# Two of sixteen dBu products moved from VectorE to GpSimd, and from PSUM to SBUF

## The reference

```python
deltaA = jnp.exp(delta[..., None] * A)                      # 16 units per channel
deltaB_u = delta[..., None] * Bm[:, :, None, :] * xi[..., None]
def step(state, inputs):
    dA_t, dBu_t, C_t = inputs
    state = dA_t * state + dBu_t
    y_t = jnp.einsum('bdn,bn->bd', state, C_t)
    return (state, y_t)
```

## Time and profile before

| | |
|---|---|
| median of 3 runs | 1354.28 us (1354.16 to 1357.81) |
| the profiled execution | 1355.75 us, span 1353.9 us |
| PE busy in the span | 1060.0 us (78%) |
| DVE busy | 932.1 us (69%) |
| POOL busy | 817.2 us (60%) |
| ACT busy | 745.8 us (55%) |
| state space, scans from 535.0 to 1020.9 us | 256 scans, mean 1204 ns |
| dBu products, line 1630 | 256, mean 685 ns |
| products with C on POOL, line 1569 | 256, mean 1273 ns |

### The profile page before, as it was taken

The page is one execution under the profiler, slowest core; times in us unless marked ns, Lnnn a source line. Parts: engine busy times, 40 slices in busy tenths (PEclk is TensorE's granted clock), DMA queues, the critical chain, the costliest instruction groups (busy, mean ns, idle before and its releaser), DMA issues. The chain is left out here.

```text
span 1353.9 us, 20321 instructions
## 1 busy us (share of the span) xinstructions
PE 1060.0 (78%) x4202; PEld 618.8 (46%) x4203; DVE 932.1 (69%) x2276; ACT 745.8 (55%) x1821; POOL 817.2 (60%) x602
## 2 busy tenths in 40 slices
PE   3898874349999955888989888897775319999995
PEld 3666653227777731333333333333223215555563
DVE  4999997503333333799999999989997625555573
ACT  3777754325555547858586776757531115555542
POOL 1443320667317557877886888788781567437276
PEclk9999985569999976989999999899897559999997
DMA  8994000136425425344435443443540026535335
GB/s 243 161 147 139 1 1 1 41 53 88 71 56 89 84 31 110 85 141 133 155 116 168 124 157 124 137 159 114 185 140 1 31 54 94 85 73 96 79 67 103
DMA packets 136875, 133.22 MB, mean 98 GB/s; under 512 B 14578, under 2 KB 117602, under 8 KB 136674
## 3 DMA queue, kind: packets, MB, share of 16 engines
q1 hardware_dynamic: 107106, 115.55, 32.3%
q0 software_dynamic: 29696, 16.86, 9.8%
HBM read 98.66 MB, written 31.60 MB: 96 GB/s over the span
## 5 line engine op out<-in xcount | busy, mean ns | idle before, releaser
L1569 POOL TENSOR_TENSOR ss_HC<-ss_Hs,ss_Cb 128x512 f32<-128x512 f32 x256 | 317.8, 1273 | 92.1 <-PE ss_Y L1343 70.9
L1343 PE MATMUL ss_Y<-ss_HC,g_ident 128*128 128x512 f32 x512 | 268.7, 643 | 45.5 <-POOL ss_HC L1569 38.0
L1638 DVE TENSOR_TENSOR_SCAN ss_Hs<-ss_dA,ss_dBu 128x512 f32<-128x512 f32 x256 | 297.3, 1204 | 7.0 <-ACT ss_dA L1485 7.0
L992 PE MATMUL m_x_UP<-g_m_w,m_x_gT 128*128 (+1 forms) x532 | 203.9, 489 | 5.9 <-issue 2.9
L1485 ACT ACTIVATE ss_dA<-ss_delta,g_A 128x510 f32<-128x510 f32 x256 | 168.0, 714 | 55.3 <-DVE ss_Hs L1638 54.9
L1343 PEld LDWEIGHTS ss_Y<-ss_HC,g_ident 128*128 128x128 f32 x512 | 90.4, 197 | 206.7 <-POOL ss_HC L1569 147.9
L1630 DVE TENSOR_TENSOR ss_dBu<-ss_duP,ss_Bb 128x512 f32<-128x512 f32 x256 | 163.4, 685 | 21.0 <-DMA ss_Bb<-bc_rows 16.8
L1012 PEld LDWEIGHTS m_x_DP<-g_m_w,m_x_hT 128*128 128x128 f32 (+1 forms) x908 | 131.0, 189 | 80.4 <-issue 41.2
L1012 PE MATMUL m_x_DP<-g_m_w,m_x_hT 128*128 (+3 forms) x908 | 161.5, 296 | 5.9 <-ACT m_x_hT L1068 3.4
L1095 DVE SCALAR_TENSOR_TENSOR m_x_hid<-m_x_UP,m_x_G,m_x_sg 128x352 f32<-128x352 f32 x78 | 45.5, 584 | 151.2 <-ACT m_x_sg L1050 147.6
L972 POOL DMA_INDIRECT g_X<-out_rows,g_slot x64 | 99.2, 1550 | 78.4 <-DMA out_rows<-m_x_YO 55.8
(11 more groups left out here) (242 smaller groups left out, 1869.8 us busy)
## 6 DMA issues: line engine op xcount, KB each, us to landing
ss_Bb<-bc_rows SPq DMA_DIRECT2D x64, 512.0 KB, 4.9
ss_Cb<-bc_rows SPq DMA_DIRECT2D x64, 512.0 KB, 4.1
rows<-g_Z SPq DMA_DIRECT2D x2, 5031.0 KB, 54.2
m_x_G<-rows SPq DMA_DIRECT2D x156, 64.5 KB
out_rows<-m_x_YO SPq DMA_DIRECT2D x156, 64.0 KB
g_m_w<-in_w_up SPq DMA_DIRECT2D x1, 2816.0 KB, 10.7
g_m_b<-in_b SPq DMA_DIRECT2D x1, 2160.0 KB, 11.2
g_X<-in_x SPq DMA_DIRECT2D x4, 512.0 KB, 5.8
```

The source lines that it names most:

```text
L992: ins = nc.tensor.matmul(UP[v % 2][:, at:at + n], gT[v % 2][:], w.w[:, ds(e + c, n)], start=True, stop=True)
L1343: ins = nc.tensor.matmul(Yp[:, h, :], ident[:], HC[n % 2][:, h, :], start=False, stop=n == N - 1)
L1569: nc.gpsimd.tensor_tensor(HC[n % 2][:, h, :], Hs[n % 4][:, h, :], Cb[g % 2][:, n % 2, :], ALU.mult).then_inc(hc_ready.sem, 1)
L1638: v_.tensor_tensor_scan(Hs[n % 4][:, h, :], dA[n % NA][:, h, :, :].rearrange("p s t -> p (s t)"), dBu[:, h, :], 0.0, ALU.mult, ALU.add).th ...
```

## The change

For the units n = 1 and n = 3 of each chunk POOL makes the product of `du` and B, from `du` in SBUF into new SBUF tiles `dBs[0]` and `dBs[1]`, with a new semaphore `shared`. DVE leaves out its products for these units and its scans read `dBs`. On POOL the product for unit 3 stands behind HC of unit 0, the one for unit 1 of the next chunk behind HC of unit 14 (for chunk 0 ahead of the first chunk). SP's waits count 14 units on `dBu_ready` and, for g = 2 and 3, `shared` as well.

```diff
+        def own(n):
+            return 2 * (n - (n > 1) - (n > 3))
...
-                        sp.wait_ge(dBu_ready.sem, dBu_ready.after(c, 2 * (2 * g - 2)))
+                        sp.wait_ge(dBu_ready.sem, dBu_ready.after(c, own(2 * g - 2)) if g else dBu_ready.after(c - 1, own(N - 2)))
+                    if g in (2, 3):
+                        sp.sem_inc(sp_passed, 1)
+                        sp.wait_ge(shared.sem, shared.after(c, 2 * (g - 1)))
...
+                def share(n, c):
+                    pool.wait_ge(b_loaded[n // 2].sem, b_loaded[n // 2].after(c, 16))
+                    if n == 1:
+                        pool.wait_ge(du_ready.sem, du_ready.after(c))
+                    for h in range(2):
+                        nc.gpsimd.tensor_tensor(dBs[n // 2][:, h, :], du[:, h, :], Bb[n // 2][:, 1, :], ALU.mult).then_inc(shared.sem, 1)
...
+                        if n == 0:
+                            share(3, c)
                         if back and 3 <= n < 7:
+                            if n == 6:
+                                pool.wait_ge(shared.sem, shared.after(c))
                             softplus_step(pool, nc.gpsimd, n - 3, c + 1, 1 - v)
+                        if n == N - 2 and back:
+                            share(1, c + 1)
+                share(1, 0)
                 chunks(pool, scan)
...
+                            if n in (1, 3):
+                                continue
...
-                            dve.wait_ge(dBu_ready.sem, dBu_ready.after(c, 2 * n + h + 1))
-                            v_.tensor_tensor_scan(Hs[n % 4][:, h, :], dA[n % NA][:, h, :, :].rearrange("p s t -> p (s t)"), dBu[:, h, :],
+                            if n in (1, 3):
+                                dve.wait_ge(shared.sem, shared.after(c, n + h))
+                            else:
+                                dve.wait_ge(dBu_ready.sem, dBu_ready.after(c, own(n) + h + 1))
+                            v_.tensor_tensor_scan(Hs[n % 4][:, h, :], dA[n % NA][:, h, :, :].rearrange("p s t -> p (s t)"),
+                                                  dBs[n // 2][:, h, :] if n in (1, 3) else dBu[:, h, :],
```

More of the change, by code:

```diff
@@ L1205, in state_space @@
         c_loaded = [m.sig(f"c_loaded{q}", 16 * N // 4) for q in range(2)]
-        dA_ready, dBu_ready, scanned = m.sig("dA_ready", 2 * N), m.sig("dBu_ready", 2 * N), m.sig("scanned", 2 * N)
+        dA_ready, dBu_ready, scanned = m.sig("dA_ready", 2 * N), m.sig("dBu_ready", 2 * (N - 2)), m.sig("scanned", 2 * N)
+        shared = m.sig("shared", 4)
+        dBs = [m.sb(f"dBs{k}", [P, 2, CH]) for k in range(2)]
         hc_ready, summed = m.sig("hc_ready", 2 * N), m.sig("summed", N)
@@ L1467, in copy_du @@
                         if at(c, 0, 1):
-                            act.wait_ge(dBu_ready.sem, dBu_ready.after(c - 1, 2 * N - 1 + h))
+                            act.wait_ge(dBu_ready.sem, dBu_ready.after(c - 1, 2 * (N - 2) - 1 + h))
                         nc.scalar.activation(duP[:, h, :], du[:, h, :], ACT.Copy).then_inc(du_copied.sem, 1)
```

## The result

The changed kernel took 1372.81 us (median; 1371.34 to 1379.55) against 1354.75 for the kernel before, a ratio of 1.0139 (95% interval 1.0124 to 1.0154): 18 us slower. The forecast was 1380.7, with a range of 1361 to 1399. The profiled execution of the changed kernel took 1372.19, its span is 1370.4 (before 1353.9), so 16.5 us of it are in the traces.

What follows compares the result with a forecast made beforehand. A loop of waits over POOL and TensorE, not VectorE, was taken as the bound. Start +7.55, first passage +1.1, five passages +17.35 and tail +0.4 made +26.4 us, a median of 1380.7 us, range 1361 to 1399.

Steps and rivals of the forecast that it cites:

- five passages: Chunk-to-chunk passages 1 to 2 up to 5 to 6: each 3.47 us longer, +17.35 us together.
- start of chunk 0: From POOL's release by its gathers to unit 3's C product: 16.97 us instead of 9.41, +7.55 us.
- passage 0 to 1: From chunk 0 to chunk 1, where POOL was waiting for DVE: about +1.1 us from scans meeting POOL products.
- tail: From unit 12 of chunk 6 on: 2.36 us saved against waits of 2.33 and 0.4 for POOL's products, +0.4 us.
- What VectorE saves: Four dBu products, 2.36 us a chunk: worth 0 in chunks 1 to 5, beside the loop, and -2.36 in the tail.
- The 2.85 us for the C load of g=2: In SP's queue this load waits for unit 1's C product, 2.85 us later; unit 6's B rows stay covered by 1 us.
- The products: Two new POOL pairs of 2.465 us, 4.93 a chunk, fit alone into 6.03 us of idle time, 1.10 to spare.
- The hold: Each of four scans a chunk with two SBUF inputs holds POOL 1.16 us, the scan's own length: 4.64 a chunk.
- From HC3 on nothing changes: In middle chunks, from unit 3's C product to the next chunk's unit 11 one, the time stays unchanged: 0.
- (a): Rival: POOL isn't held by the scans; passages cost 0, +0.4 us in all, 1354.7 us; chance 0.12.
- (d): Rival: only one of two scan pairs collides with POOL; 1.22 us a passage, start about +5, 1365 us; chance 0.07.
- (c): Rival: POOL keeps the port through a whole gapless run; +6.5 us a passage, about +45, 1399 us; chance 0.06.

Runs made afterwards that it cites:

- e5: Kernel before with HC as a ring of four places instead of two, without the change: 1335.15 us, ratio 0.9858 to the kernel before.
- e1: Changed kernel, but scans of units 1 and 3 read old values in PSUM while GpSimd still makes both products: 1353.48 us, ratio 0.9984 to the kernel before.
- e2: Changed kernel, but GpSimd makes neither product and scans of units 1 and 3 read an SBUF tile set once: 1355.85 us, ratio 0.9995 to the kernel before.
- e8: Changed kernel with the product moved for unit 1 alone, unit 3's back on VectorE: 1365.51 us, ratio 1.0088 to the kernel before.
- e11: Changed kernel with its ring of two, ScalarE copying GpSimd's two products into PSUM for the scans: 1365.31 us, ratio 1.0066 to the kernel before.
- e7: Changed kernel with the product moved for unit 3 alone, unit 1's back on VectorE: 1355.84 us, ratio 1.0006 to the kernel before.
- e6: Changed kernel with HC as a ring of four places instead of two: 1351.79 us, ratio 0.9988 to the kernel before.

## Why the prediction was right, and where its sizes were off

The mechanism is the one forecast: a loop over POOL and TensorE (e5), a gap in it that takes either cost but not both (e1, e2), and a port that makes a scan and a POOL product wait for each other. The Trainium skill, page "SBUF — State Buffer", section "Who interferes with whom", has it that a VectorE instruction with two SBUF inputs contends with GpSimd's reads, that the shared pair is an exclusive lock and that issue order decides who blocks; its sentence on the whole instruction is about VectorE's 2-port modes. The stretched scans and products agree with it in kind, though POOL's loss per scan is 0.92 us and less than the scan, and the three long waits of the last section are not told by issue order.

By the terms of the sum, read at the start of HC3 in each chunk (the last column gives the time or the stretch before and after; the five passages are from HC3 of chunk 1 to that of chunk 6):

| term | forecast | measured | from |
|---|---|---|---|
| start of chunk 0 | +7.55 | +6.13 | 561.35, 567.48 |
| passage 0 to 1 | +1.1 | +2.47 | 64.46, 66.93 |
| five passages | +17.35 | +8.55 | 298.62, 307.17 |
| tail | +0.4 | -0.9 | 96.70, 95.77 to HC15 of chunk 7 |
| sum | +26.4 | +16.2 | |

**What VectorE saves** was right: nothing in the middle, and it stays off the path. Its waits for B rows are larger in sum (19.1 us against 16.8), not in every chunk: before unit 12 of chunks 2 and 3 they are 2.61 and 1.80 us where they were 1.72 and 1.24, but of chunk 4 1.63 where it was 1.96. The 2.85 us for the C load of g=2 left out the held scans: the load goes out 25.8 us behind HC11 instead of 19.4, the cover of 1 us is gone and VectorE waits 0.52 us for the B rows of unit 6, in its own slack as said.

**The products** were right: 2.465 us a pair, and 1.16 us to spare in e1 against 1.10. What the sum doesn't hold is that a delay can also act through TensorE: in e8 product and hold together are 4.3 us, less than the 6.03 of POOL's idle time, and still a passage grows, by the wait for the second half of HC15.

**The hold** was the first term mis-sized: 0.92 us and not 1.16, nearer to the 0.97 of the earlier trace rows than to the scan's length that I took. With it the formula gives 24.65 + 3.68 = 28.33 from HC11 to HC3; measured are 28.24 (before 25.77), +2.47 a passage. At the start it gives 16.01 from POOL's release, and 15.96 are measured; POOL was also released 0.4 us earlier.

**"From HC3 on nothing changes"** was the step that failed. From HC3 to the next HC11 the kernel before took 33.39 to 35.09 us, 33.95 in the mean, and the changed one 33.12 to 33.22. The chunk that I had followed (33.59) has no wait before HC5. Those on both sides of it have one of 0.58 us, and the one after these 1.89:

```profile
695.15 2.51 POOL L1569 TENSOR_TENSOR ss_HC<-ss_Hs,ss_Cb 128x512 f32<-128x512 f32 x2 [0.58 <-PE ss_Y L1343]
...
875.10 2.51 POOL L1569 TENSOR_TENSOR ss_HC<-ss_Hs,ss_Cb 128x512 f32<-128x512 f32 x2 [1.89 <-PE ss_Y L1343]
```

These are rows of the kernel before, HC5 in two chunks. POOL waits there for the sum of unit 3, behind the output and ScalarE's gate copy. Whether it waits goes with TensorE's clock in the output. Here are the outputs of the chunk that I followed (granted clock 1.00) and of the one with 1.89 us (0.50), both of the kernel before:

```profile
749.17 2.05 PE L1329 MATMUL ss_Q<-g_w_out,ss_yg 128*128 128x128 f32 x16 [2.96 <-ACT ss_gate L1425]
...
868.32 3.75 PE L1329 MATMUL ss_Q<-g_w_out,ss_yg 128*128 128x128 f32 x16 [3.06 <-ACT ss_gate L1425]
```

In the changed kernel TensorE waits 2.0 us for the gate copy and the output takes 2.02 to 2.05 us in all five passages; POOL comes 2.4 us later to HC5 and never waits. Its lateness alone would nearly do: in e11, where the output starts at about the same distance from HC11 and is slow each time, HC5 starts 37.7 to 38.0 us behind HC11, and in the changed kernel 37.7 to 37.8. So a second wait, parallel to the first, had been there anyway. Five times 2.47 less five times 0.75 are about the 8.55; the waits before HC5 are 0.61 of the 0.75, shorter ones before HC10 0.10.

**Passage 0 to 1** was under-sized: the gate is DVE's own there, and TensorE's wait for it brought slow rows, which I had not counted. It is unit 1's scans that do it: +4.4 us in e8, 0.0 in e7, -1.2 in e1.

**The tail** gained 0.9 where I had +0.4. Without the held scans (e1) it gains 2.2, near the 2.36 that VectorE saves; with them but without POOL's products (e2) 0.95. So the held scans cost it 1.3 us, where I had 2.73 of waits.

The range's upper sum is a little off in itself: four holds of 1.28 and one product make 5.18 a passage and not 5.25. Of the rivals, (a) is what e1 shows once the scan reads PSUM, (d) is e2's and e7's unit 3, and something near (c) happens, but seldom: twice in e6 and once in e8. By the traces the sum is 10 us too high: 5.0 by the hold in the five passages, 3.8 by the stretch from HC3 on, 1.4 by the start and 1.3 by the tail, less 1.4 for passage 0 to 1.

## What to carry to other kernels

Before moving an elementwise product from VectorE to GpSimd, look at where the consumer will read it: here a scan that had one SBUF operand and then had two made both engines wait for each other (0.92 us for GpSimd and mostly up to 1.0 for VectorE per scan), while a copy by ScalarE into PSUM kept the gain once the ring had four places, and with the ring of two did not. And look first for a loop of waits between the engines: a busy share of 95% on VectorE was no bound, the ring of two buffers was, and opening it gave 1.4% where moving work gave a loss. When two delays share one gap, each alone can be free and the two together not; and a delay can be partly free because another wait runs beside it, so follow more than one chunk round.

## What the runs showed of the hardware that I had not expected

- **How the two engines share.** A scan of two SBUF operands issued while a GpSimd product runs starts when this ends: 740.58 to 742.48 in the changed kernel, 1.90 us for the first of the pair and 2.22 for the second, with one product of 2.18 us (1.26 alone) between. They take turns, instruction by instruction. In 3 of 192 such scans (all runs together, about 155 of them issued while GpSimd was busy) the scan was passed over by one to three further products, and stood for 3.33 (e8), 5.71 and 5.78 us (e6). All three were issued 0.24 to 0.30 us after a product with C had begun, but one in e2, at 0.30, was not passed over, nor were two at 0.24 and 0.26 behind the start of a product of `du` and B. What decides it stays open.
- **TensorE's clock.** In passage 0 to 1 of the changed kernel TensorE waits 1.97 us for the gate, and the next rows run at the lower level: the D product takes 3.58 us, against 1.98 where there is no such wait. The granted clock of the stretch is 0.66 in the mean, so part of it at 1.2 instead of 2.4 GHz, and 1.00 on both sides of it. A wait of 1.75 us (e8) was followed by 3.14 us, one of 1.40 (e2) by 3.05, one of 0.86 (e7) by 1.98. The timeline's row:

```profile
625.42 3.58 PE L1349 MATMUL ss_Y<-ss_xi,ss_w_D 128*128 128x512 f32 x4 [1.97 <-DVE ss_yg L1636]
```

The stretches around it (columns of the earlier trace rows, the clock is the first after POOL's):

```profile
619.00:625.00 6.00, 4.45 (x10) 1.34 (x8) 6.00 (x5) 4.11 (x8) 6.00 (x4) 1.00 0.58 176
625.00:630.00 5.00, 4.58 (x7) 2.03 (x8) 5.00 (x6) 4.92 (x7) 2.80 (x3) 0.66 0.25 71
630.00:636.00 6.00, 6.00 (x16) 2.66 (x15) 6.00 (x8) 5.96 (x8) 4.08 (x4) 1.00 0.35 130
```

Here the wait of 1.97 us and the 1.60 by which the product is longer are 3.57 us of TensorE's time; the passage as a whole grew by 2.47. The same wait need not have the same price: the two outputs above follow waits of 2.96 and 3.06 us and take 2.05 and 3.75.
